# The list by time counts TensorE's streaming lengths plus a time for each change of tiling, and prefers the running tiling

## The reference, cut to what matters

```python
x = x + L0_attn(layernorm(x)) + L0_ffn(layernorm(x))
xn = layernorm(x)
scores = einsum('bihd,bjhd->bhij', q, k) * DH ** -0.5      # 16 heads of 16
attn = softmax(where(causal, scores, -inf))
seq_out = einsum('bhij,bjhd->bihd', attn, v)
...                                                        # incidence memory, gate
h = gelu(xn @ (W1 + scale * m1[b]).T + b1)
x = x + (seq_out + gated * mem_val) @ out_w + out_b + h @ (W2 + scale * m2[b]).T + b2
```

## Time and profile before

| | us |
|---|---|
| median of 3 runs (lowest, highest) | 4015.3 (4014.3, 4017.3) |
| profiled execution, span | 4018.3 |
| TensorE busy in it | 3760.5 (94%) |
| VectorE busy | 3169.5 (79%) |
| ScalarE busy | 2658.1 (66%) |
| GpSimd busy | 2253.1 (56%) |

### The profile page before, as it was taken

How to read it: one execution, slowest core, us unless ns; L and a number is a source line. 1 busy time by engine, 2 the same in 40 slices (tenths; PEclk the granted TensorE clock), 3 DMA queues, 4 the chain that set the end, 5 groups by cost and what they waited for, 6 DMA issues and landing times.

```text
span 4018.3 us, 61587 instructions
## 1 busy us (share of the span) xinstructions
PE 3760.5 (94%) x19488; PEld 2328.4 (58%) x19488; DVE 3169.5 (79%) x6074; ACT 2658.1 (66%) x4142; POOL 2253.1 (56%) x1756
## 2 busy tenths in 40 slices
PE   7999998999999999998889999999999999999997
PEld 3656655656555565665555555565555656556564
DVE  3788999989999999999676775867758677695863
ACT  6778778777887878786345565565555655556555
POOL 4787998988999989998541321413214132141411
PEclk9999999999999999999799999999999999999999
DMA  4445554444555545555321222212222122131111
GB/s 154 125 149 168 157 164 150 156 159 154 169 159 169 157 150 162 167 167 170 124 88 36 73 73 65 75 47 72 65 65 78 52 73 65 57 96 58 57 46 28
DMA packets 251029, 442.07 MB, mean 110 GB/s; under 512 B 25860, under 2 KB 80596, under 8 KB 249812
## 3 DMA queue, kind: packets, MB, share of 16 engines
q1 hardware_dynamic: 250708, 438.14, 35.4%
HBM read 366.39 MB, written 69.21 MB: 108 GB/s over the span
## 4 chain that ended last, share of the span: by engine, by line
PE 52%; DVE 11%; ACT 7%; issue 6%; POOL 1%; DMA 1%; SPq 0%; DVEq 0%; ACTq 0%; POOLq 0%
PE ps L1521 6%; PE ps L1420 6%; PE ps L1529 6%; PE ps L1382 4%; PE ps L1401 4%; PE ps L1451 3%; PE ps L1457 3%; PE ps L1283 3%; PE ps L1333 2%; DVE ps L1921 2%; PE ps L1293 2%; DVE ps L1943 2%; PE ps L1462 1%; PE ps L1428 1%; PE ps L1277 1%
## 5 line engine op out<-in xcount | busy, mean ns | idle before, releaser
L2167 POOL TENSOR_TENSOR drive<-du,b_wide 128x1024 f32<-128x1024 f32 x512 | 1202.1, 2363 | 202.0 <-DVE held L1921 119.5
L2202 POOL TENSOR_SCALAR_AFFINE_SELECT exps<-exps 128x256 f32<-128x256 f32 x512 | 223.2, 439 | 1132.7 <-ACT exps L1546 1129.0
L1546 ACT ACTIVATE exps<-ps 128x1024 f32<-128x1024 f32 (+3 forms) x768 | 619.2, 810 | 341.8 <-PE ps L1401 318.9
L1546 ACT ACTIVATE ps<-delta,neg_a 128x512 f32<-128x512 f32 x1024 | 681.8, 685 | 151.1 <-DVE heavy L1899 137.0
L1943 DVE CUSTOM_DVE_ANT_0 ps<-ps,later 128x128 f32<-128x128 f32 (+3 forms) x1024 | 484.5, 512 | 219.5 <-PE ps L1382 209.8
L1333 PE MATMUL ps<-p_all,heavy 128*128 128x128 f32 x3072 | 443.0, 281 | 71.6 <-DVE heavy L1899 64.6
L1333 PEld LDWEIGHTS ps<-p_all,heavy 128*128 128x128 f32 x3072 | 364.4, 144 | 242.8 <-DVE heavy L1899 119.9
L1899 DVE TENSOR_TENSOR heavy<-c_wide,ps 128x512 f32<-128x512 f32 x704 | 468.1, 671 | 8.2 <-issue 4.1
L1921 DVE TENSOR_TENSOR_SCAN ps<-ps,carry,drive 128x512 f32<-128x512 f32 x352 | 441.6, 1273 | 32.5 <-ACT ps L1546 32.3
L1921 DVE TENSOR_TENSOR_SCAN ps<-ps,drive 128x512 f32<-128x512 f32 x352 | 420.3, 1214 | 49.9 <-ACT ps L1546 47.7
L1946 DVE TENSOR_REDUCE smax<-ps 128x2 f32<-128x1024 f32 x256 | 311.9, 1218 | 107.3 <-PE ps L1382 95.3
(11 more groups left out here) (197 smaller groups left out, 6568.7 us busy)
## 6 DMA issues: line engine op xcount, KB each, us to landing
b_wide<-bc_dram SPq DMA_DIRECT2D x512, 256.0 KB, 3.4
c_wide<-bc_dram SPq DMA_DIRECT2D x512, 256.0 KB, 3.5
stacks<-parts SPq DMA_DIRECT2D x192, 256.0 KB, 2.4
qs<-stacks SPq DMA_DIRECT2D x128, 192.0 KB
ks<-stacks SPq DMA_DIRECT2D x128, 192.0 KB, 4.3
x_row<-in_x SPq DMA_DIRECT2D x14, 1024.0 KB, 7.6
resid<-mix SPq DMA_DIRECT2D x9, 1024.0 KB, 5.4
x_row<-resid SPq DMA_DIRECT2D x9, 1024.0 KB, 5.4
```

The source lines that it names most:

```text
L1546: return nc.scalar.activation(out_, in_, func, **kw)
L2167: G.tensor_tensor(drive[:, g % DRIVE_SLOTS, :, :], du[:, e, :, :], wide(b_wide[:, g % B_SLOTS, :], MD), ALU.mult).then_inc(driven, 1)
```

## The change

The planner alone is changed. (1) Lengths become pure streaming times. (2) Each layer-1 unit on TensorE has a mode: `rows` (`sm`, `st`), `columns` (`pv`), `parts` (`e1`, `e2`) or `whole`; all of layer 0 is `whole`. A unit whose mode differs from that of the last one starts `TURN` + `FIRST` later in the plan (0.207 us, 0.13 for columns); one of the same mode that had to wait pays `FIRST`. (3) On TensorE a layer-1 task is chosen by start plus `DRIFT` (0.056 us) per tick, no longer by start with the tick for ties. A `rows` unit that would follow another mode gets `SHORT` (0.2 us) more when no bank pair is free. Each engine now puts forward its own first choice, and the one with the earliest start is booked. (4) Places: `LEAD` 21, other `SPANS`, `LAYER1_FROM` 1110.

```diff
@@ -434,15 +434,21 @@
 DENSE_BANKS = ([3], [0], [1], [4], [5], [6], [7])
 PARTNER = {0: 1, 1: 0, 4: 5, 5: 4, 6: 7, 7: 6}
 PV_BANK = 2
-SCORES = {P: 0.26, 2 * P: 0.32, 3 * P: 0.37, HALF: 0.43}
-LENGTH = {"xt": 0.55, "qk": 1.8, "pa": 1.6, "pb": 1.35, "lt": 0.5, "jw": 0.6, "fw": 0.5, "fr": 0.5, "ms": 0.5,
-          "zt": 0.55, "wo": 1.8, "e1": 0.47, "e2": 0.47, "f1": 1.85, "o": 3.55}
+SCORES = {P: 0.13, 2 * P: 0.13, 3 * P: 0.18, HALF: 0.23}
+LENGTH = {"xt": 0.44, "qk": 1.72, "pa": 1.56, "pb": 1.22, "lt": 0.44, "jw": 0.89, "fw": 0.44, "fr": 0.44, "ms": 0.44,
+          "zt": 0.44, "wo": 1.72, "e1": 0.23, "e2": 0.23, "f1": 1.72, "o": 3.44}
 EMPTY_A = {"xt": 0.61, "qk": 0.69, "pa": 0.55, "pb": 0.24, "lt": 0.6, "jw": 0.49, "zt": 0.6, "f1": 0.8, "mt": 0.27}
 EMPTY_V = {"qk": 0.75, "pa": 0.6, "pb": 0.43, "fw": 1.42, "fr": 0.75, "ms": 0.22, "e1": 0.75, "e2": 0.75, "o": 0.42,
            "wo": 0.68, "mt": 0.28, "ot": 1.1}
-LEAD = 20
+LEAD = 21
 LAG = 5
-SPANS = {"early": (-40, -30), "late": (-24, 8), "second": (-12, 24), "mlp": (20, 74), "close": (4, 30)}
+SPANS = {"early": (-46, -27), "late": (-24, 8), "second": (-2, 31), "mlp": (22, 74), "close": (4, 36)}
+
+
+def values_length(jt, ch):
+
+    widths = [exp_width(t, ch) for t in out_tiles(jt, ch)]
+    return 0.04 + max(sum(widths[0::2]), sum(widths[1::2])) / 600
 
 
 def layer1_tasks():
@@ -491,7 +497,7 @@
                 ("s", "stack", g) if n == 0 else None)
             add("v", unit, 0.18 + width / 492, first + n - LEAD, ("p",) + unit)
         place["mt", g] = first + UNITS - LEAD
-        add("p", ("mt", g), 0.27, place["mt", g], ("v", "sm", g, NT - 1, NC - 1))
+        add("p", ("mt", g), 0.11, place["mt", g], ("v", "sm", g, NT - 1, NC - 1))
         add("a", ("mt", g), EMPTY_A["mt"], place["mt", g], ("p", "mt", g), ("s", "maxima", g - 1) if g else None)
         add("v", ("mt", g), EMPTY_V["mt"], place["mt", g], ("a", "mt", g))
         add("s", ("maxima", g), 1.2, place["mt", g], ("v", "mt", g), late=2.0)
@@ -506,11 +512,11 @@
                 add("g", ("select",) + unit[1:], 0.41, tick, ("a",) + unit)
             if out_tiles(jt, ch):
                 turned = ("a", "turn") + ((g, 0) if ch else (g - 1, NC - 1))
-                add("p", ("pv",) + unit[1:], 0.08 + sum(exp_width(t, ch) for t in out_tiles(jt, ch)) / 1180, lag,
+                add("p", ("pv",) + unit[1:], values_length(jt, ch), lag,
                     ("a",) + unit, last, ("v", "pa", b, jt), turned if (jt, ch) in ((TC - 1, 0), (1, 1)) and g + ch else None)
             if jt == TC * (ch + 1) - 1:
                 add("a", ("turn", g, ch), 0.6, lag, ("p", "pv") + unit[1:], ("p", "ot", g - 1) if g and not ch else None)
-        add("p", ("ot", g), 0.9, first + UNITS + LAG, ("a", "turn", g, NC - 1))
+        add("p", ("ot", g), 0.87, first + UNITS + LAG, ("a", "turn", g, NC - 1))
         add("v", ("ot", g), EMPTY_V["ot"], first + UNITS + LAG, ("p", "ot", g), ("g", "join", g - 1) if g else None)
         add("g", ("join", g), 1.35, first + UNITS + LAG, ("v", "ot", g), ("v", "gate", b, NC - 1))
 
@@ -615,6 +621,17 @@
     return now
 
 
+MODES = {"sm": "rows", "st": "rows", "pv": "columns", "e1": "parts", "e2": "parts"}
+FIRST = {"whole": 0.107, "rows": 0.107, "columns": 0.03, "parts": 0.107}
+TURN, DRIFT = 0.1, 0.0560
+SHORT, RUN = 0.200, 1
+
+
+def mode_of(unit):
+
+    return MODES.get(unit[1], "whole") if unit[0] == "L1" else "whole"
+
+
 def by_time(tasks, choices, pool_of, opens):
 
 
@@ -635,7 +652,7 @@
             followers[a].append(name)
     open_tasks = {e: {n: None for n in tasks if n[0] == e and not missing[n]} for e in "pavgs"}
     free, orders, banks = {e: 0.0 for e in "pavgs"}, {e: [] for e in "pavgs"}, {}
-    used, bank_free = {}, {n: 0.0 for n in range(8)}
+    used, bank_free, mode = {}, {n: 0.0 for n in range(8)}, "whole"
 
     def from_when(choice):
         return max([choice[0]] + [bank_free[n] for n in choice[1]])
@@ -644,17 +661,34 @@
         best = None
         soonest = {pool: min(from_when(choice) for choice in choices[pool]) for pool in choices}
         for e in "pavgs":
+            first = None
+            waiting = sum(name[1] == "L1" and name[2] in ("sm", "st") for name in open_tasks[e]) if e == "p" else 0
             for name in open_tasks[e]:
                 start = max(ready[name], free[e])
                 if name in needs:
                     start = max(start, soonest[pool_of(name[1:])])
-                choice = (start, tasks[name][1], name)
-                if best is None or choice[:2] < best[:2]:
-                    best = choice
+                key = start
+                if e == "p":
+                    own = mode_of(name[1:])
+                    if own != mode:
+                        start = max(start, free[e] + TURN) + FIRST[own]
+                    elif name[1] == "L1" and start > free[e]:
+                        start += FIRST[own]
+                    if name[1] == "L1":
+                        key = start + DRIFT * (tasks[name][1] - LAYER1_FROM)
+                        if own == "rows" and mode != own:
+                            free_pairs = sum(from_when(one) <= start for one in choices["wide"])
+                            key += SHORT * max(0, RUN - min(free_pairs, waiting))
+                choice = (key, tasks[name][1], name, start)
+                if first is None or choice[:2] < first[:2]:
+                    first = choice
+            if first and (best is None or (first[3], first[1]) < best[:2]):
+                best = (first[3], first[1], first[2])
         start, _, name = best
         length, _, _, late = tasks[name]
         end, e, unit = start + length, name[0], name[1:]
         if e == "p":
+            mode = mode_of(unit)
             end = at_pace(used, start, length, SHARES.get(unit[1] if unit[0] == "L1" else unit[0], 1.0))
         del open_tasks[e][name]
         free[e] = end
@@ -681,7 +715,7 @@
     return orders, banks, max(free.values())
 
 
-LAYER1_FROM = 1140
+LAYER1_FROM = 1110
 
 
 def all_tasks():
```

## The result

The changed kernel takes 3992.1 us in the median (3989.5 to 3996.2, 4 runs) against 4014.8 for the kernel before: ratio 0.9948, 95% interval 0.9934 to 0.9962. That is faster by 22.7 us, 0.5%, where 63 us were forecast. The profiled spans are 3987.8 and 4018.3, 30.5 us apart, 7.8 more than the medians: executions of one kernel differ (the four of the kernel before took 4011.1 to 4017.3, those of the changed one 3989.5 to 3996.2), and a span is that of one execution, from its first instruction to its last.

What follows compares the result with a forecast made beforehand. TensorE alone was taken to bound the 2150 to 3950 us stretch, changes of tiling being its largest cost that isn't work. Only the preference counted: 4018.3 - 63 = 3955 us span, 3952 median, other terms 0; range 3885 to 4010.

Steps and rivals of the forecast that it cites:

- the reading of a visit's fixed time: TensorE, layer-1 stretch: fixed 0.21 us per scores visit, 0.19 per whole-array visit; one round trip costs 0.40 us.
- Layer 0's list unchanged until the crossing: Layer 0: one mode, no change time booked, list the same until layer 1's first tasks open near 1900 us; 0.
- 0 for the crossing itself: Crossing from layer 0 to layer 1, 1900 to 2150 us: places may advance attention or delay layer 0; 0, from -20 to +15.
- I take the mean, 63 us: Layer-1 stretch: preference for the running tiling saves round trips; mean of 74 and 52 us, ends 0 and 118.
- The count from the banks: Ends of scores runs: 450 of 763 had a pair read out; 186 round trips fewer, 74 us.
- The count from the ticks: Steps from whole array to scores: about 35% had a near dense unit; 129 round trips fewer, 52 us.
- I count 0 net: Scores' tiling, all pairs full: plan holds TensorE idle up to 0.49 us, but saves a 0.40 round trip; 0.
- All this moves work in the full stretch ... 0: New LEAD and spans: they shift work in the stretch where TensorE's sum is what counts; 0.
- at 0 in itself: New lengths in the plan: its clock agrees with the chip, which lets the preference work; priced at 0.
- No gain: the pairs, not the choice, set the runs: Rival, chance 0.13, scores runs: saved changes are paid back as waits for a read-out; 4005 to 4020 us.
- Held idle in the scores' tiling: Rival, chance 0.11: third and later scores units of a run wait 0.35 us idle, costing 105 us against 63; 4057.
- Theory E: From the follow-up runs, not the prediction: the whole list's mesh sets the time; median 58 to 65 us above planned end.

Runs made afterwards that it cites:

- e6: The changed kernel with the start of the MLP units' span moved by one tick, from 22 to 23: 4024.4 us, ratio 1.0024.
- e9: The changed kernel with DRIFT = 0, so the running tiling is kept whenever that saves time at once, whatever the ticks: 4374.5 us, ratio 1.0891.
- e3: The changed kernel with the old LEAD, SPANS and LAYER1_FROM: 4032.8 us, ratio 1.0046.
- e4: The changed kernel with RUN = 2: entering scores from another tiling costs 0.2 us more in the choice unless two bank pairs are free; 4025.4 us, ratio 1.0019.
- e8: The changed kernel with other places (early, late, mlp spans; LAYER1_FROM 1100), chosen for a small planned end, and SHORT 0.05: 3966.9 us, ratio 0.9878.
- e14: The changed kernel with places chosen under the old rule (early -43 to -25, late -23 to 10, second 3 to 25, mlp 21 to 72): 4068.9 us, ratio 1.0145.
- e11: The changed kernel with the start of the late units' span moved by one tick, from -24 to -23: 4009.0 us, ratio 0.9985.
- e13: The changed kernel with TURN, FIRST and DRIFT at 0: streaming lengths, nothing for a change of tiling, the old choice; 4136.0 us, ratio 1.0302.
- e2: The kernel before with the new LEAD, SPANS and LAYER1_FROM, but no new lengths and no preference: 4023.8 us, ratio 1.0014.
- e5: The changed kernel with TensorE's tasks chosen as before, the time of a change of tiling only booked: 4034.3 us, ratio 1.0039.
- e10: As e5 (change time booked, no preference for the running tiling), with other places chosen for a small planned end: 4013.6 us, ratio 0.9996.

## Why the prediction was right or wrong

**Right.** The sign, with luck in it: the same rule with one span one tick later (e6) is 0.24% slower than the kernel before. TensorE as the bound, and the reading of a visit's fixed time: it returns after (0.33 for a first unit of 512, 2711.24 to 2711.57; 0.23 for a continuing one). That a continuing unit pays no weight load (before, the loads for the one at 3958.37 run from 3958.15 for 0.19 us, beside the matmuls of the unit ahead) holds for other widths too: the shortest distances of starts in e9 are 0.057, 0.116, 0.173 and 0.229 us for 128, 256, 384 and 512 columns, in proportion to the columns, with nothing fixed beside them. Layer 0's list unchanged until the crossing (the 8 us between the two executions there are scatter), and 0 for the crossing itself: what the rule moves forward there it pays for at the end of layer 0.

**Wrong, the step that carries the sum: "I take the mean, 63 us" from the two counts of round trips.** 158 fewer were expected, from changes 1605 to about 1290. The changes fell by 144, some 72 round trips, 29 us (in the counted stretch to 1466). This term alone is 34 of the 40 us that are missing.
- The count from the banks (450 of 763 ends of a run with a pair free) used read-out times of the chip. But the list is made in the plan's clock. Replaying the old planner with a note at each end of a scores run: of 825 ends, 278 had no scores unit open at all, in 56 one could have started at once, in 95 more within 0.207 us, in 396 only later. At equal ticks the preference could keep 151 runs going, not 450.
- The count from the ticks assumed that a near dense unit is open. Whole-array visits fell by 80 where 129 were counted.

**Wrong: "I count 0 net" for the idle that the new key accepts.** In the changed kernel little was paid back, 22.5 of 29 us arrived, and the idle time named before scores units grew by 10.8. Elsewhere it is much larger: e3 saves 75 more changes than the changed kernel and loses 41 us, e4 105 and loses 33. In both, half-clock time and idle rose by 27 to 62 and 25 to 35 us. The prediction's sum had no term for the clock at all. Time at half clock goes with 0.43 us of span per us in the fit, beside the idle time itself.

**Wrong: "All this moves work in the full stretch ... 0" for the places.** I took them as neutral, and under the new rule alone other places move the median from 3966.9 (e8) to 4068.9 (e14). One tick on one span moves the median by 17 to 32 us (e11, e6). The crossing, where 0 was taken from a range of -20 to +15, isn't part of it.

**New lengths "at 0 in itself".** Alone they cost 112 us (e13 against e2); with the time of a change beside them they are still 10 us slower than the old lengths at the same places (e5 against e2), and at places of its own e10 equals the kernel before (0.9996). They had to come together, and together they gain nothing that a run shows.

**The rivals.** "No gain: the pairs, not the choice, set the runs" named a mechanism that e3, e4 and e14 show: TensorE's waits at scores units for a pair sum to 66.6, 63.9 and 64.8 us there, 40.6 before. The 22.7 us are those of one list, rule and places together. "Held idle in the scores' tiling" is what e9 does (such waits 203 us), not the changed kernel: there a scores unit of 512 columns between two others took 0.42 us in the mean at full clock, where before it took 0.60.

**What stays open.** Which waits make one list 60 us better than a neighbour wasn't followed unit by unit. Whether the rule would win with equally long searches for both isn't settled: the best planned ends found were 3906 with the new rule and 3925 with the old, and the old rule's list was 24 us worse on the chip than Theory E had it. The planner is also no independent witness of the clock: in both kernels it books streaming at half pace behind a stretch of little use (`at_pace`), a rule that no run here tests, and whether a better model of this would help wasn't tried.

## What to carry to other kernels

When a greedy planner writes the order, a change of its rule or of one constant draws a new list, and lists of the same rule lie 1% or more apart; before a gain is put down to a rule, run both rules at several settings. Here the planner's own end time told more than the count of changes that the rule was meant to reduce: 13 of the 18 kernels measured 54 to 66 us above it, and four of the others 45 to 90, but a plan whose lengths leave out a real cost (e13, 348 above) tells nothing and yields bad lists. Count opportunities in the clock of whoever decides, here the plan's, not the chip's.

## What the runs showed of the hardware

TensorE's busy time holds more than streaming. It includes the tails: the `o` group lasts 3.72 us, but the next unit starts 3.65 after it. Matmuls that overlap count once: 1414 of 412 ns in the mean would be 583 us, and 293.5 are booked. And it includes the changes of tiling: between 2702.82 and 2723.27 us of the kernel before there are 16, and TensorE is busy for 20.45 of 20.45 us, while a scores unit of 512 columns takes 0.34 or 0.31 us beside a change and 0.22 without one.

A scores unit that follows a scores unit starts the next one after 0.057 us per 128 columns (e9, shortest of each width: 0.057 to 0.229 us), so neither a weight load nor anything else fixed is added; a first one of 512 columns takes 0.33 (changed kernel, 2711.24) to 0.34 (before, 2711.19).

The clock fell to half (0.50 from 3014.53 to 3016.82) after a stretch in which TensorE was busy for 2.64 of 4 us with four waits of 0.19 to 0.47 us (e9, 3010 to 3014), and stayed at 1.00 (3022.34 to 3023.55) after one in which it was busy for 2.00 of 3 us with waits of 0.20 to 0.69 (3020 to 3023). Over the 18 profiles the half-clock time behind the first scores unit ranges from 61 to 485 us, and each microsecond of it goes with 0.43 us of span. That is near what `pv` shows in e9: sixteen matmuls took 2.29 us at a clock of 0.50 and 1.21 at 1.00, so 0.47 us lost per us at half clock.

The same list doesn't take the same time: up to the unit that all 18 lists share it took 1955.0 to 1964.6 us. A difference of a few us between two profiled executions, or a unit that comes earlier, is no effect of a change before it is compared at a point where both have done the same work.
